# Two graph-attention blocks on one core: VectorE takes each step's mask ahead of the newest scores' maximum, ScalarE the high part ahead of their eviction

## The reference, cut to what matters

```python
def _gat_layer(x, W, adj):
    proj = x @ W
    Wh, Ws = jnp.split(proj, 2, axis=-1)
    scores = Wh @ Ws.T
    a = jax.nn.softmax(scores, axis=-1) * adj
    out = a @ Wh
    out = out + x
    return jax.nn.leaky_relu(out, NEG_SLOPE)
```

## Time and profile before

| | |
|---|---|
| median of 3 runs | 1577.26 us (1576.45 to 1577.85) |
| the profiled execution, its own time | 1576.58 us |
| its span | 1574.8 us |
| TensorE matmul busy | 1542.0 us, 98% |
| VectorE busy | 1138.9 us, 72% |
| ScalarE busy | 1067.3 us, 68% |
| GpSimd busy | 969.6 us, 62% |

### The profile page before, as it was taken

The page is one execution under the profiler, slowest core; times in us unless marked ns, Lnnn a source line. Parts: engine busy times, 40 slices in busy tenths (PEclk is TensorE's granted clock), DMA queues, the critical chain, the costliest instruction groups (busy, mean ns, idle before and its releaser), DMA issues.

```text
span 1574.8 us, 34791 instructions
## 1 busy us (share of the span) xinstructions
PE 1542.0 (98%) x12902; PEld 1532.8 (97%) x12902; DVE 1138.9 (72%) x2145; ACT 1067.3 (68%) x2085; POOL 969.6 (62%) x864
## 2 busy tenths in 40 slices
PE   6999999999999999999999999999999999999998
PEld 5999999999999999999999999999999999999997
DVE  7766666666666577778777778766777777777774
ACT  4579889988985566666666666645666666666666
POOL 2112222222220288888888888846888888888885
PEclk9999999999999999999999999999999999999999
DMA  4124444454441034344444435522343344434343
GB/s 151 48 61 118 125 115 119 119 147 120 115 115 35 24 95 105 105 105 106 107 108 105 105 105 161 204 68 75 105 105 105 105 105 105 105 105 105 105 107 106
DMA packets 95034, 166.27 MB, mean 106 GB/s; under 512 B 12816, under 2 KB 25743, under 8 KB 94607
## 3 DMA queue, kind: packets, MB, share of 16 engines
q1 hardware_dynamic: 66816, 116.17, 27.2%
q0 software_dynamic: 24336, 44.31, 11.5%
q10 hardware_dynamic: 3710, 3.56, 0.7%
HBM read 150.87 MB, written 13.13 MB: 104 GB/s over the span
## 4 chain that ended last, share of the span: by engine, by line
PE 89%; issue 3%; DVE 3%; POOL 2%; ACT 1%; DMA 1%; SPq 0%; POOLq 0%; DVEq 0%; ACTq 0%
PE PS L1295 33%; PE PS L1507 9%; PE PS L1510 9%; PE PS L1509 9%; PE PS L1370 5%; PE PS L1367 5%; PE PS L1369 5%; PE PS L1368 5%; PE PS L1366 5%; POOL FR L508 1%; POOL X L501 1%; DVE ROW L837 0%; DVE AF L1104 0%; DMA X<-xt 0%; PE PS L1538 0%
## 5 line engine op out<-in xcount | busy, mean ns | idle before, releaser
L508 POOL TENSOR_TENSOR FR<-AF,FR 128x512 fp32r<-128x512 f32 x338 | 451.1, 1335 | 122.3 <-ACT FR L703 114.6
L1295 PE MATMUL PS<-FR,RB 128*128 128x256 f32 x3900 | 514.0, 281 | 1.8 <-ACT X L657 1.7
L1295 PEld LDWEIGHTS PS<-FR,RB 128*128 128x128 f32 x3900 | 481.9, 188 | 3.0 <-ACT X L657 3.0
L501 POOL TENSOR_TENSOR X<-X,ROW 128x512 f32<-128x512 f32 x283 | 370.7, 1310 | 82.0 <-ACT ROW L713 82.0
L1507 PE MATMUL PS<-FR,RA 128*128 128x256 f32 x1300 | 370.6, 285 | 2.5 <-POOL FR L508 2.3
L1510 PE MATMUL PS<-FR,RA 128*128 128x256 f32 x1300 | 365.0, 281 | 0.0
L1509 PE MATMUL PS<-FR,RA 128*128 128x256 f32 x1300 | 364.4, 280 | 0.0
L1104 DVE TENSOR_TENSOR AF<-PS,AJ 128x512 f32<-128x512 f32 x338 | 231.0, 683 | 56.3 <-ACT PS L669 46.2
L466 POOL DMA_DIRECT2D STGT<-adjt x169 | 90.1, 533 | 293.0 <-PE PS L1370 293.0
L1036 DVE TENSOR_TENSOR AF<-PS,AF 128x512 f32<-128x512 f32 x286 | 196.4, 687 | 100.7 <-PE PS L1295 98.4
L657 ACT ACTIVATE X<-PS 128x512 f32<-128x512 f32 x272 | 162.3, 597 | 156.4 <-DVE AF L1036 149.5
(11 more groups left out here) (174 smaller groups left out, 2424.1 us busy)
## 6 DMA issues: line engine op xcount, KB each, us to landing
AJ<-adjt SPq DMA_DIRECT2D x338, 256.0 KB, 2.7
STGT<-adjt POOLq DMA_DIRECT2D x169, 256.0 KB, 3.0
xt_scratch<-ROW SPq DMA_DIRECT2D x12, 512.0 KB, 2.6
RB<-xt_scratch SPq DMA_DIRECT2D x12, 512.0 KB, 6.2
x_scratch<-X ACTq DMA_DIRECT2D x13, 256.0 KB, 2.1
ROW<-x_scratch SPq DMA_DIRECT2D x13, 256.0 KB, 3.3
out<-ROW SPq DMA_DIRECT2D x12, 256.0 KB, 3.5
ROW<-rec_scratch SPq DMA_DIRECT2D x22, 128.0 KB, 3.7
```

What stands on the lines that cost most here:

```text
L501: nc.gpsimd.tensor_tensor(slot, slot, MB.unsqueeze(1).broadcast_to([P, 2, 256]), ALU.subtract)\
L508: nc.gpsimd.tensor_tensor(LO[g % 2], WA[g % 2], HI[g % 3].bitcast(F32), ALU.subtract)\
L1295: last = nc.tensor.matmul(out, stationary(a, k), moving(b, k), start=(k == 0 and i == 0), stop=(k == K - 1 and i == 2))
```

## The change

In the ScalarE loop `high(x)` moves ahead of `evict(e)`; in the VectorE loop `mask(x)` moves to the head of the step, ahead of `maximum(e)` and of `weighted`. No instruction is added or removed, and every wait stays with its instruction.

```diff
@@ -794,10 +794,10 @@
                     keep_rec(A_END[v - 1])
                 if x is not None and x < GL:
                     exponent(x)
+                if x is not None:
+                    high(x)
                 if e is not None:
                     evict(e)
-                if x is not None:
-                    high(x)
                 z = A_AT.get(v + 3)
                 if z is not None and z >= GL:
                     row_exponent(z)
@@ -1226,12 +1226,13 @@
             wh_low(5)
             for v in range(STEPS):
                 x, e = A_AT.get(v + 1), S_AT.get(v - 1)
+
+                if x is not None:
+                    mask(x)
                 if e is not None:
                     maximum(e)
                 if R_END.get(v - 1) is not None and v - 1 != LAST1:
                     weighted(R_END[v - 1])
-                if x is not None:
-                    mask(x)
                 if R_END.get(v - 1) is not None and v - 1 != LAST1:
                     residual(R_END[v - 1], 0)
                 if e == NG - 1:
```

## The result

The changed kernel takes **1589.32 us** (median of 4 runs, 1588.39 to 1590.38), the kernel before 1577.45 (4 runs, 1576.45 to 1577.85). The ratio is 1.0078, 95% interval 1.0062 to 1.0094. The forecast of 1585.2 us, slower, had the sign and the range (1581 to 1591) right; the middle was 4.1 us too low, and the time lies 0.7 us above 1588.6, the upper end of the forecast's own bounds. The profiled execution is the one of 1590.38 us, with a span of 1588.6 us against 1574.8.

The account below looks back on a forecast made before the run. TensorE bounds the kernel, busy 1542.0 of 1574.8 us. 7.8 + 0.8 + 0.6 - 0.8 - 0.5 = 7.9 us on 1576.58 gives 1584.5, plus 0.7 to the median: 1585.2 us; range 1581 to 1591.

Parts of the forecast that it names:

- the seam: Step after a block's last scores: copy and eviction stand behind waiting mask, 0.34 us at each of 23, 7.8 us.
- rival 1: Delays not caught up, scores at block ends stall: 0.3 to 0.8 us in seven blocks, 1587 to 1591; chance 0.14.
- The ring: Ordinary step: exponent, mask, maximum, eviction, next exponent take 2.54 us, below TensorE's 2.86, so no time is lost.
- Rival 2: Weights for the held scores load early, so each seam costs 0.23 us, 5.3 instead of 7.8, 1582.7 us; chance 0.08.
- The DRAIN rule: Between VectorE instructions: next waits for empty pipe, 0.68 between starts, would give 0.42 a seam, 9.7 us; trace disagrees.
- The weight split: Where VectorE comes late out of splitting the second layer's weights: maximum and eviction start behind the mask, +0.8 us.
- Block ends: Later inversion delays the reload by about 0.4 us, tight in seven blocks that wait for it; counted zero.
- The layer boundary: Between the layers: eviction at 1075.39 instead of 1073.98, TensorE 1.4 later, less a 0.65 wait gone, +0.6 us.
- Gifts: Earlier low parts at block ends, three waits gone, -0.8 us; last row maximum earlier, 0.47 us wait gone, -0.5 us.
- The sign to look for: Profile after: TensorE waiting for ScalarE's eviction (L657, and L659) some 23 times, about 0.2 to 0.3 us each.

Follow-up runs that it names:

- experiment 1: Changed kernel with the old order of mask and high part in the steps where keep_max is issued: 1581.15 us, ratio 1.0029.
- experiment 3: Changed kernel with ScalarE's exponent ahead of keep_max in the step that issues keep_max: 1579.29 us, ratio 1.0018.
- experiment 6: Changed kernel with layer 1's leaky replaced by a maximum of one PSUM and one SBUF input, layer 2's kept: 1588.49 us, ratio 1.0068.
- experiment 2: Kernel before with one half of the change alone: VectorE's mask first, 1651.46 us, ratio 1.0477; ScalarE's high part first, 1586.11 us, ratio 1.0063.
- experiment 4: Changed kernel with ScalarE's exponent ahead of keep_max and also ahead of keep_rec: 1578.85 us, ratio 1.0007.
- third kernel of experiment 7: Kernel before with the new order only in the first 91 steps (exponent ahead of keep_max and keep_rec) and behind the last scores: 1575.31 us, ratio 0.9990.

## Why the prediction was right, and where it was off

The mechanism of the largest term, the seam, is right and shown by removal. That the range held the time is owed to rival 1, which stretched it from 1588.6 to 1591; by its own terms alone the forecast would have missed by 0.7 us.

- **The ring.** Right. Mask to mask is 2.45 us where the changed kernel catches up at the boundary (1083.63, 1086.08), against 2.54 worked out; the eviction gives ScalarE to the exponent after 0.50, not 0.60. With TensorE's step at 2.86 an ordinary step costs nothing; experiments 1 and 3 show it.
- **The seam, 23 x 0.34 = 7.8.** Right, 0.33 each, 7.5. The copy came 0.60 behind the mask, the eviction 0.72 behind the copy, TensorE 0.05 behind its end.
- **Rival 2, the head start kept (0.23 a seam).** Wrong. By the Trainium skill (TensorE: Matmul & The Clock Gate, Architectural detail: the array is 16× 32×32) the weight load could have gone ahead; at 697.83 load and matmul start together. The further 0.10 shows at the next scores.
- **The DRAIN rule (0.42 a seam).** The trace still does not agree with the strict reading: copy behind mask 0.60, both 0.68 long. The section that the prediction cites (the Trainium skill, VectorE: DVE Perf Modes, The DRAIN you can't avoid) itself adds that an instruction which is not held starts earlier, and with that the trace agrees; the prediction passed over it.
- **The weight split, +0.8.** Sized too low: 1.3. The prediction had VectorE come to the split as before. Its two instructions took 2.5 us before (957.59 to the maximum of the earlier trace rows at 960.06) and 2.2 after, but began late. The first of them, in the kernel before, after the change, and in experiment 6 without the held `leaky`:

```profile
957.59 0.84 DVE L1264 TENSOR_TENSOR WX<-ROW,WX 128x512 fp32r<-128x512 f32 x1 [1.14 <-ACT WX L816]
```

```profile
962.96 1.63 DVE L1265 TENSOR_TENSOR WX<-ROW,WX 128x512 fp32r<-128x512 f32 x1 [1.11 <-ACT WX L816]
```

```profile
962.47 1.62 DVE L1267 TENSOR_TENSOR WX<-ROW,WX 128x512 fp32r<-128x512 f32 x1 [1.10 <-ACT WX L816]
```

Against the offset that TensorE has there (4.55 and 4.85) the split begins 0.8 us late after the change and on time in experiment 6, where the place costs 0.5. A `leaky` held at 949.30 for 1.48 us, 14 us earlier, is what the ring had not caught up. Experiment 1 begins the split 0.92 late and loses 1.4 there, experiment 3 0.36 late and loses 0.85: each time the lateness and some 0.5. So the step that failed is "VectorE comes out of the split" at an unchanged time, and the +0.8 was itself too much for a split that begins on time.

- **Block ends, counted at zero.** This is the step that failed. "I count zero" held for the 22 ordinary ends, tight as they were, and failed for the last block but one of layer 1, by 2.7 us. The prediction had looked for `keep_max` alone as an instruction that waits for TensorE ahead of an exponent. `keep_rec` does the same in the steps where a block is finished at once, and the 0.3 us a step of reserve are too few for both within three steps. Some 0.8 of the 2.7 are its held `leaky` (experiment 6). Rival 1 (the reserve is spent) happened, at this one block, for 2.7 us where it was priced at 2 to 5.6 in seven.
- **The layer boundary, +0.6.** Right where the clock stays up: in experiment 3 the offset rises by 1.43 and falls by 0.90, +0.53. In the profiled execution of the change it is 2.0.
- **Gifts, -0.8 and -0.5.** Here -0.6 and -1.3. The three waits for the low part went as counted; but at the loop's start the new order first costs 0.3 (545.09) of the 0.4 that the first one gives back, and the third lies in the last block but one and is counted there. At the end not only the 0.47 of the earlier trace rows went, but also a wait of 1.7 us for L679 further on, with 0.5 for `leaky` in its place, which the prediction did not follow.
- **The sign to look for, 23 waits for L657 with 0.2 to 0.3 us each.** Right, but only in the list of the weight loads: 23 of its 31 waits lie at seams, 0.26 to 0.30 each. The matmuls' own list has six, since modelled matmul ends cover the short ones. The prediction did not say which list.

Against the forecast's terms the profiled execution has 2.7 more at the last block but one, 0.5 more at the split, 0.6 more gained and 0.3 less at the seams, together +2.3; the boundary's clock adds 1.5, the clock near 105 us another 1.5, and 0.7 were not followed up. The measured difference of medians is 11.9 where 7.9 was forecast; how many of the other executions had such stretches of low clock is not on record. The comparison is loose by about 1 us: the changed kernel's four runs go from 1588.39 us at a mean granted clock of 1.000 to 1590.38 at 0.996.

## What to carry to other kernels

Before an instruction is moved behind one that waits, list everything that is queued ahead of that one's producer on the other engine, under every branch of the loop; here both faults were an exponent behind a readout that waits for TensorE. The cure that cost nothing was there, in the producer's queue, and not in the order that was changed. A ring of handoffs shorter than the bounding engine's step costs nothing in an ordinary step (2.45 us against 2.86), one longer by 0.1 us costs at every step and at every disturbance besides. And short waits of TensorE are to be looked for at its weight loads.

## What was not expected of the hardware

**A hold between VectorE and GpSimd.** A VectorE instruction with both inputs in SBUF that starts while a GpSimd instruction is in flight takes 1477 ns instead of 686, or 1080 instead of 425, and one with one of its two inputs in PSUM is not held (experiment 6). In the changed kernel 23 of the 25 `leaky` start 0.37 us into a GpSimd instruction and are held; the other two start beside none and take 700 and 680 ns. It makes up VectorE's 40 us: the durations of `leaky` grow by 18.3 us, those of L1120 (23 held) by 15.1, those of L1051 (11 held) by 10.2. It goes the other way too: in the changed kernel the GpSimd instruction that starts behind a held one takes up to 1.8 us instead of 1.3, and in the kernel before `low`, which started 0.2 us behind `leaky`, took 1.6. The Trainium skill (SBUF — State Buffer, Who interferes with whom) says that the two engines share a pair of ports which only one of them has at a time, and that an instruction of VectorE with two SBUF inputs contends with a GpSimd instruction that reads SBUF; which one blocks is decided by who comes first. This case's traces agree. Before the change all 25 `leaky` came first (685 to 700 and 677 to 679 ns); the new order lets the high part, and so `low`, start ahead of nearly all of them. The prediction overlooked the rule. With layer 1's `leaky` out of it, the two steps of 0.8 us in the trace are gone.

**The clock behind a wait.** TensorE and the granted clock (the third figure from the right of a stretch's row) at the layer boundary of the changed kernel:

```profile
1085.60 2.93 PE L1296 MATMUL PS<-FR,RB 128*128 128x256 f32 x12 [2.57 <-ACT X L657]
```

```profile
1084.00:1088.00 4.00, 2.40 (x11) 2.40 (x12) 3.40 (x6) 2.89 (x6) 2.94 (x3) 0.68 0.32 77
1088.00:1092.00 4.00, 4.00 (x33) 4.00 (x33) 2.92 (x5) 2.49 (x5) 3.79 (x4) 0.89 0.41 121
```

And the same place in experiment 3:

```profile
1079.70 1.68 PE L1299 MATMUL PS<-FR,RB 128*128 128x256 f32 x12 [2.59 <-ACT X L657]
```

```profile
1078.00:1082.00 4.00, 2.30 (x19) 2.30 (x20) 3.44 (x6) 2.79 (x6) 2.84 (x3) 1.00 0.29 74
```

After 2.57 us without work the twelve matmuls took 2.93 us, part of them at 1.2 GHz, and the next scores came 1.5 us later than in experiment 3, where TensorE had idled 2.59 us and the clock stayed at 2.4 GHz. The profiles of experiments 1 and 2 show 2.93 us there too, behind waits of 2.50 to 2.58 us; those of experiments 4 and 6 show 1.68 us behind waits of 2.57. So the wait alone does not decide; what does stays open.

It is also most of why work that no kernel here changes puts the loop's start later in one execution than in another. The same stretch of it before and after the change:

```profile
106.00:109.00 3.00, 3.00 (x27) 3.00 (x27) 1.91 (x4) 3.00 (x7) 0.53 (x1) 1.00 0.12 20
```

```profile
106.00:109.00 3.00, 3.00 (x16) 3.00 (x15) 1.91 (x4) 3.00 (x7) 0.47 (x1) 0.50 0.04 8
```

TensorE is busy throughout both, but at 1.2 GHz it gets through 16 matmuls instead of 27, and its offset goes from 0.05 us at 104 us to 1.53 at 110. Nine of the twelve profiles have such a stretch there and lose 1.4 to 1.5 us by it; those of the kernel before, of experiment 1 and of the third kernel of experiment 7 have none. What sets it off is open, as are the other differences ahead of the loop, up to 1.3 us (experiment 4).
